# Turning the residual within quads of partitions, and carrying the quads across by DMA

## The reference

```python
# block A, t = condB_t: scale, shift from t by small matrices
out = silu(scale * _layer_norm(x, gamma, beta) + shift)      # norm over positions and features
out = out @ W_in + b_in
out = silu(scale * _layer_norm(out, gamma, beta) + shift)
x2 = out @ W_out + b_out + x
# block B, expert e = itok[b]: H 512, I 2048
h = gelu(x2 @ Wi[e] + bi[e])
r = h @ Wo[e] + bo[e] + x2
y = (r - mean(r)) * rsqrt(var(r) + 1e-12) * gamma[e] + beta[e]   # norm over features
```

## Time and profile before

| | us |
|---|---|
| median of 3 runs | 1762.91 |
| lowest and highest run | 1762.43, 1763.22 |
| profiled execution, its own time | 1762.18 |
| its span in the trace | 1760.2 |
| PE / VectorE / ACT busy | 1749.2 / 1466.8 / 1053.8 |
| transposes of the residual on VectorE | 256, 179.9 busy |
| granted TensorE clock | 0.999 of full speed |

### The profile page before, as it was taken

One profiled execution on the slowest core, in us unless ns is written; L12 is line 12 of the kernel. 1 busy time (PEld: TensorE's weight loads), 2 busy tenths in 40 slices (PEclk: granted clock), 3 DMA queues, 4 the chain that ended last, 5 costly groups with the idle time before them and its releaser, 6 DMA issues.

```text
span 1760.2 us, 25797 instructions
## 1 busy us (share of the span) xinstructions
PE 1749.2 (99%) x8947; PEld 1482.3 (84%) x8947; DVE 1466.8 (83%) x2471; ACT 1053.8 (60%) x1699; POOL 88.6 (5%) x137
## 2 busy tenths in 40 slices
PE   9999999999999999999999999999999999999998
PEld 6888888888888888888888888888888888888887
DVE  7987979888798887978879788797888879888585
ACT  5766556565655656556665566655666556565543
POOL 1000000000000000000000000000000000000000
PEclk9999999999999999999999999999999999999999
DMA  6332423324233242332323324243242433323231
GB/s 258 99 100 76 139 95 97 122 76 146 77 116 114 77 136 87 123 102 98 120 74 123 111 96 124 65 134 99 97 135 63 138 97 96 123 76 123 84 132 60
DMA packets 71555, 189.57 MB, mean 108 GB/s; under 512 B 13955, under 2 KB 18051, under 8 KB 71300
## 3 DMA queue, kind: packets, MB, share of 16 engines
q1 hardware_dynamic: 62642, 183.95, 32.6%
q10 hardware_dynamic: 8786, 3.99, 1.3%
HBM read 171.10 MB, written 16.81 MB: 107 GB/s over the span
## 4 chain that ended last, share of the span: by engine, by line
PE 76%; DVE 14%; ACT 5%; issue 4%; DMA 1%; SPq 0%; DVEq 0%; ACTq 0%; POOL 0%
PE out_acc L641 31%; PE hid_ps L641 29%; PE blk_ps L730 14%; ACT work L899 2%; DVE work L1195 2%; DVE h_lo L1109 1%; DVE g_lo L1109 1%; PE blk_ps L641 1%; ACT L882 1%; DVE wo_lo L1109 1%; DVE wi_lo L1109 1%; DVE x_turned L1347 1%; DVE work L1205 1%; ACT g_hi L886 1%; DMA cond_a<-in_cond_w 1%
## 5 line engine op out<-in xcount | busy, mean ns | idle before, releaser
L641 PE MATMUL hid_ps<-x_hi,wi_hi 128*128 128x512 f32 x1020 | 399.8, 392 | 0.4 <-DVE wi_lo L1109 0.3
L641 PE MATMUL hid_ps<-x_lo,wi_hi 128*128 128x512 f32 x1020 | 398.2, 390 | 0.0
L641 PE MATMUL out_acc<-wo_hi,g_hi 128*128 128x512 f32 x1012 | 394.9, 390 | 3.0 <-DVE x_turned L1371 2.9
L641 PE MATMUL hid_ps<-x_hi,wi_lo 128*128 128x512 f32 x1020 | 396.9, 389 | 0.0
L641 PE MATMUL out_acc<-wo_hi,g_lo 128*128 128x512 f32 x1012 | 393.9, 389 | 0.0
L641 PE MATMUL out_acc<-wo_lo,g_hi 128*128 128x512 f32 x1012 | 393.8, 389 | 0.0
L882 ACT ACTIVATE g_sb<-hid_ps,bi_sb 128x512 f32<-128x512 f32 x256 | 175.6, 686 | 219.2 <-PE hid_ps L641 214.0
L1109 DVE TENSOR_TENSOR g_lo<-g_sb,g_hi 128x512 fp32r<-128x512 f32 x253 | 172.2, 681 | 127.3 <-ACT g_hi L886 125.8
L840 ACT ACTIVATE wo_hi<-stage 128x512 fp32r<-128x512 f32 x253 | 159.8, 632 | 146.8 <-PE out_acc L641 126.3
L641 PEld LDWEIGHTS out_acc<-wo_hi,g_hi 128*128 128x128 f32 x1012 | 190.0, 188 | 47.5 <-issue 8.5
L641 PEld LDWEIGHTS hid_ps<-x_hi,wi_lo 128*128 128x128 f32 x1020 | 191.5, 188 | 40.8
(11 more groups left out here) (202 smaller groups left out, 2437.4 us busy)
## 6 DMA issues: line engine op xcount, KB each, us to landing
stage<-in_expert_w SPq DMA_DIRECT2D x256, 512.0 KB, 3.5
x<-in_xT SPq DMA_DIRECT2D x64, 256.0 KB, 3.3
out_y<-x_turned SPq DMA_DIRECT2D x63, 256.0 KB, 3.2
rows<-in_expert_rows SPq DMA_DIRECT2D x16, 512.0 KB, 4.6
mv_all<-mv_dram ACTq DMA_DIRECT2D x30, 128.0 KB, 3.4
affine_sb<-in_affine SPq DMA_DIRECT2D x3, 512.0 KB, 9.7
w_raw<-in_W SPq DMA_DIRECT2D x2, 512.0 KB, 6.3
w_raw<-in_W_in SPq DMA_DIRECT2D x4, 256.0 KB, 9.7
```

Source lines behind the costliest of these rows:

```text
L641: last = pe.matmul(dst, w[wp], xs[xp], start=start and i == 0, stop=stop and i == 2)
```

## The change

Features are laid out anew by the host. A permutation `FEATURES` is applied to every array with a feature axis of the model's width, on the side that the kernel reads, so that partition quad h of chunk c holds features 128 h + 32 c to 128 h + 32 c + 31. The rows of output of block B keep their order, so `Wo`, gamma, beta and y are as before.

VectorE turns all 128 partitions of a chunk with one instruction, `turn(b, c)`: each of the four quads is turned within its own 32 partitions, 16 blocks of 32x32 each, into `half_turned`. Four such instructions per batch stand in ticks 6 and 7, two in each (batch 0: all four in tick 3). After that quad h holds positions in its partitions and the 128 features of the same quad side by side, 512 bytes. `bring_turned(b)` has SP issue 16 transfers from SBUF to SBUF, one for each pair of quads (h, s): 32 partitions x 4 position tiles x 512 bytes, 64 KB. They write `x2_turned`. They stand after block 11 in SP's queue (batch 0: after block 7).

`half_turned` has the same memory as `h_hi`. It is written once the first product of block A of the next batch is done, and ACT's first write of `h_hi` after it (`rounded` of `A11_B11` at tick 10, in batch 0 `h_hi_part` at tick 6) waits for the sixteen transfers. So does the rounding of the last batch at its tick 10, and `r_evac`. The wait for the stores of y moves from VectorE's turn to SP's `bring_turned`, and the load of x waits for 4 turns instead of 16.

```diff
-TURN_AT = {5: (0, 3), 6: (3, 8), 7: (8, 12), 8: (12, 14), 9: (14, 16)}
-TURN_AT_0 = {2: (0, 3), 5: (3, 4), 7: (4, 8), 8: (8, 12), 9: (12, 16)}
+TURN_AT = {6: (0, 2), 7: (2, 4)}
+TURN_AT_0 = {3: (0, 4)}
...
+FEATURES = np.arange(D).reshape(P // BLOCK, DC, BLOCK).transpose(1, 0, 2).reshape(D)
...
+        with ExitStack() as at_h:
+            half_turned = at_h.enter_context(nc.sbuf_tensor("half_turned", [P, S // BLOCK, DC, BLOCK], F32))
         h_hi = sb("h_hi", [P, DC, S], F32R)
...
                 if b >= 2:
-                    sp.wait_ge(s_turn, len(QUADS) * (b - 1))
+                    sp.wait_ge(s_turn, DC * (b - 1))
...
+            def bring_turned(b):
+
+                sp.wait_ge(s_turn, DC * (b + 1))
+                if b >= 1:
+                    sp.wait_ge(st_y, 16 * ST * b)
+                else:
+                    sp.wait_ge(s_wlo[1], 2)
+                for h, s in QUADS:
+                    src = half_turned[BLOCK * h:BLOCK * (h + 1), s::P // BLOCK].rearrange("p t c i -> p t (c i)")
+                    sp.dma_start(x2_turned[BLOCK * s:BLOCK * (s + 1), :, P * h:P * (h + 1)], src) \
+                      .then_inc(ld_turned, 16)
...
                     load_block(HT * b + j, expert)
+                    if j == (7 if b == 0 else 11):
+                        bring_turned(b)
...
                 act.wait_ge(s_silu, DC * turn_of(b, which) + c + 1)
+                if (b, which, c) == (1, 0, 0):
+                    act.wait_ge(ld_turned, 16 * len(QUADS))
                 copy(h_hi[:, c, :], work[:, c, :]).then_inc(s_hhi, 1)
...
+                if i == A11_B11 and which:
+                    act.wait_ge(ld_turned, 16 * len(QUADS) * b)
...
                     act.wait_ge(s_eye, 1)
+                    act.wait_ge(ld_turned, 16 * len(QUADS) * B)
                     copy(eye, eye_raw[:, :]).then_inc(s_resthi, 1)
-                    act.wait_ge(s_turn, len(QUADS) * B)
...
-            def turn(b, q):
-
-
-                h, s = QUADS[q]
-                if q == 0:
-                    dve.wait_ge(s_bo, DC * (b + 1))
-                    if b >= 1:
-                        dve.wait_ge(st_y, 16 * ST * b)
+            def turn(b, c):
+
+                dve.wait_ge(s_bo, DC * b + c + 1)
+                if c == 0 and b + 1 < B:
+                    if b + 1 >= FIRST_SEVEN:
+                        dve.wait_ge(s_product, products_until(b + 1, 0, S4_B22))
                     else:
-                        dve.wait_ge(s_wlo[1], 2)
-                quad = lambda t, n: t[BLOCK * n:BLOCK * (n + 1)]
-                src = quad(x_sb[b % 2], h).rearrange("p c (t q j) -> p c t q j", q=P // BLOCK, j=BLOCK)
-                dst = quad(x2_turned, s).rearrange("p t (c q j) -> p c t q j", q=P // BLOCK, j=BLOCK)
-                dve.transpose(dst[:, :, :, h, :], src[:, :, :, s, :]).then_inc(s_turn, 1)
+                        dve.wait_ge(s_blk, 2 * DC * (b + 1))
+                dve.transpose(half_turned[:, :, c, :], x_sb[b % 2][:, c, :]).then_inc(s_turn, 1)
...
             def r_evac(b, s):

-                dve.wait_ge(s_turn, len(QUADS) * (b + 1))
+                dve.wait_ge(ld_turned, 16 * len(QUADS) * (b + 1))
```

More of the change, by code:

```diff
@@ L402, in build @@
         s_turn = sem("s_turn")
+        ld_turned = sem("ld_turned")
         s_r, s_rbn, s_rmv, s_rcen, s_rout = (sem(f"s_r{n}") for n in ("", "bn", "mv", "cen", "out"))
@@ L1697 @@
     E = {name[8:]: value for name, value in a.items() if name.startswith("L1_cond_")}
+    for name in ("bsc", "bsh", "b_in", "b_out"):
+        A[name] = A[name][FEATURES]
+    for name in ("Wsc", "Wsh", "W_in", "W_out", "gamma", "beta"):
+        A[name] = A[name][:, FEATURES]
+    for name in ("W_in", "W_out"):
+        A[name] = A[name][FEATURES]
+    E["Wi"], E["bo"] = E["Wi"][:, FEATURES], E["bo"][:, FEATURES]
     def columns(v):
@@ L1705 @@
     arrays = {
-        "xT": a["x"].transpose(0, 2, 1),
+        "xT": a["x"].transpose(0, 2, 1)[:, FEATURES],
         "itok": a["itok_B_0_7"],
```

## The result

| | before | after |
|---|---|---|
| median of the runs, us | 1762.96 (10 runs) | 1767.85 (10 runs) |
| lowest and highest run | 1761.83, 1763.56 | 1766.41, 1769.00 |
| profiled execution, its own time | 1762.18 | 1766.60 |
| its span | 1760.2 | 1764.6 |

The ratio is 1.0028, with a 95% interval of 1.0018 to 1.0038: the change makes the kernel 4.9 us slower. The forecast was 1763.2, no change, in a range of 1760.0 to 1769.0. The time is inside the range, but 4.65 us above the forecast, at the place of the "in-between" case that was given 0.05. It is also above 1766.4, up to which the prediction called a time "same", and its interval leaves 1 out: "no change" did not come true.

A forecast was written before the change was run, and what follows sets the result against it. TensorE (PE), busy 1749.2 of 1760.2 us, was taken as the bound, so only its waits count. The profiled 1762.18 - 2.5 (head start) + 2.8 (batch 0) = 1762.5; median 0.7 above: 1763.2 us, range 1760 to 1769.

The forecast's parts named there:

- no change: Whole kernel: forecast 1763.2 us, with any time from 1759.4 to 1766.4 us called "same"; chance 0.80.
- in-between: SP's issues 0.62 to 0.72 us apart: batch 0 pays 4.9 to 6.4 us, gain shrinks, 1765 to 1769; chance 0.05.
- Part 1, the head start: Ticks 8 and 9: without two transposes ahead, VectorE's affine step lets ticks 10 to 12 start 1.5 us sooner; 2.5 us gained.
- Rivals 2 and 3: Faster, 1757: wait at each first `down` goes too, chance 0.04; slower, 1774: 128-partition transposes cost 2.8 us each, chance 0.03.
- Part 2, the steps of SP: SP's sixteen transfers a batch, issued 0.48 us apart, land before ACT's rounding of tick 10 in batch 1 and later; cost nothing.
- The landing: From issue to landing of the sixteen transfers: 2.8 us, with 1.8 and 3.3 as ends.
- a slack of 2.1: Tick 10, batch 1 and later: transfers landed at 432.0, ACT's rounding at 434.1 with the head start; 2.1 us of slack.
- no wait of ACT for them at tick 10: Sign of being right: ACT does not wait for the sixteen transfers at tick 10 of batches 1 to 14.
- issues over 0.6 us apart: Sign of being wrong: SP's issues of the transfers stand more than 0.6 us apart, where 0.48 was taken.
- Part 3, batch 0: Batch 0: four transposes in tick 3 and the late transfers delay PE, 2.8 us in all, the 1.2 at tick 5 within it.
- Tick 5: Batch 0: four transposes push `wi_lo` of tick 4, so the `up` that needs it makes PE stop for 1.2 us.
- Tick 7: Batch 0: ACT rounds `h_hi` only after transfers land at 80.1; PE's block starts at 81.4 instead of 78.58, 2.8 us late.

The follow-up runs named there:

- the first experiment: The change in batches 1 to 15 only, batch 0 turned by 16 direct transposes as before: 1759.89 us against 1762.89 for the kernel before, ratio 0.9982.

## Why the prediction was right, and where it was wrong

**Part 1, the head start, was right.** 2.5 us was taken, with 2.7 as its end, and batches 1 to 14 gave 2.7; tick 13 of batch 0 gave another 0.2. In the medians of the first experiment it is 3.0. Part of the loss had stood in tick 11, not in tick 12 alone. Relative to the batch's first `down`, ACT's rounding of tick 10 moved from 435.56 - 382.56 = 53.00 to 440.86 - 389.32 = 51.54 us in that batch, so by 1.46, where 1.5 was forecast; where ACT waited for the transfers it moved by less. The transposes cost 0.69 us in the mean, 0.6 apart, against 0.72, VectorE is at 1333.5 against 1335, and the wait at the first `down` stayed, as the idle 3.60 us of the earlier trace rows said; it is 3.59 after. Rivals 2 and 3 are out by these rows.

**Part 2, the steps of SP, is where it failed.** The sixteen began 428.76 - 389.32 = 39.44 us after the first `down`; the forecast had 422.0 - 382.56 = 39.44. From there two terms were off. The distance of two issues was taken as 0.48 us, from the x transfers of the earlier trace rows, and was 0.644. It was argued that the number of rows sets it, and the runs showed that neither that number nor the size, the source or the dimensions do so alone. The landing was taken as 2.8 us and was 2.0, the profile's median for these transfers. Here the Trainium skill was nearer: its page DMA: Bandwidth & Descriptors, section Anatomy of one DMA, has for a transfer issued by GpSimd a fixed part of some 2.0 us and adds little for 64 KB, and the trace agrees for these, which SP issued. In the batch of the earlier trace rows that is 10.03 - 7.2 - 0.8 = 2.0 us together, which turned a slack of 2.1 into one of 0.1. In each of the five batches where ACT waited, one of the sixteen issues took 1.2 to 1.9 us instead of 0.60 (why is not shown), their starts spread over 10.2 to 11.1 us, and no slack was left. So two signs named in the prediction went against it: "no wait of ACT for them at tick 10" failed in five of the 14 batches, and issues over 0.6 us apart were a sign of being wrong. That PE still lost nothing was forecast, but not for this reason: the prediction let the gain shrink as soon as ACT waits, from 0.62 us an issue on, and the runs show ACT waiting up to 1.18 us with the gain whole.

The Trainium skill's other figure on that page, 0.95 us of engine time for 64 KB (section Bandwidth), did not add up sixteen times: the issues took 10 to 11 us, not 15.2, and DMA's share in that stretch of batch 0 was 0.55. It pointed to the right danger all the same.

**Part 3, batch 0, was right in its mechanism and short in its size.** Tick 5: 1.3 us against 1.2. Tick 7: the block was to start 2.8 us late, at 81.4, and started at 84.23, 5.65 late. The 2.8 between these are 15 x 0.164 = 2.5 for the distance of issues and 0.8 for a first gap of 1.46 instead of 0.644, less 0.8 for the landing, and 0.3 for ACT and VectorE behind it. The same mis-sized term as in part 2, and here it met no slack. Then a term was missing: the granted clock fell behind this stop, which cost 1.7 us more in the profiled execution. The sum with these sizes is 1762.18 - 2.9 + 7.2 = 1766.5, and the profiled execution took 1766.60.

**The chances.** The forecast's 0.80 for "no change" rested on one row for the distance of issues. The prediction had worked out that 0.62 us is where the case turns, 0.14 above the value taken, and had seen rows from 0.48 to 0.78; with those ends 0.05 for the in-between was too little. It gave 1765 to 1769 for that case, and the time was there, though for half of the reason: batch 0 paid (7.2 where 4.9 to 6.4 were given), while the gain did not shrink. With the 0.644 us measured, that case's own sum gives batch 0 only 70.1 + 9.7 + 2.8 + 1.3 - 78.6 = 5.3 us; the shorter landing, the longer first gap and the clock's fall were in no sum. So that the time fell inside the range is in part luck.

## What to carry to other kernels

A transfer that is issued costs the queue of its issuer, and the price must be taken from a row with the same pattern on both sides, or from both ends of the rows there are: here sixteen small transfers took 11 us of SP, and each place tried for them in the batch without slack made something else late. Busy time taken from an engine that isn't the bound is worth only what stands ahead of a waited-for instruction: one entry in a table gave the same 3 us as 133 us less work. Where an estimate puts a stop on TensorE, give the lower clock behind it a range of its own: here it cost between nothing and 2.9 us.

## What the runs showed of the hardware that was not expected

- SP's issues of transfers into `x2_turned` took 0.59 to 0.61 us each and stood 0.633 to 0.644 us apart in the median, for 64 and 256 KB, runs of 512 bytes and 2 KB, 32 and 128 partitions, and for 64 KB from SBUF and HBM; the loads of 512 KB and 256 KB from HBM took 0.33 and 0.43 us each in the same kernel. The cause is open.
- A VectorE transpose of 128 x 512 costs no more than one of 32 x 512: 687 ns against the 703 of the earlier trace rows.
- After TensorE had stood idle for 4.1 us the granted clock was 0.58 over the next 4 us, and matmuls of 512 columns started 0.427 us apart instead of 0.227, for 1.7 us in all; with useless products in the gap it stayed at 1.00. Behind two stops of the same 3.08 us, in kernels that are alike up to there, it fell once and once not.
- The broadcast of batch 0's totals lands at another time in each execution: VectorE's totals began between 61.16 and 64.04 us in the profiled ones. With the direct turns in batch 0 none of that reaches PE (no excess in tick 5 with totals from 61.72 to 62.87). With the four transposes in tick 3, PE's excess in tick 5 was 1.1 to 1.3 us with totals from 61.16 to 62.04, and 1.9 to 2.8 us with totals from 63.00 to 64.04.
- A wait of ACT for DMA transfers can stand in the list of waits as "issue": 4.1 us in five batches of the changed kernel, 77.7 us in the one with the transfers a block later, each ending 0.07 us after the last landing.
